# A layer's second attention with its exponent pass five steps behind the scores

## The reference, cut to what matters

```
h = rmsnorm(X, norm1_w)
q, k, v = (h @ wq), (h @ wk), (h @ wv)          # 16 heads of 8 features
scores = einsum('bshd,bthd->bhst', q, k) / sqrt(8)
attn = softmax(scores, axis=-1)                 # no mask here
X = X + einsum('bhst,bthd->bshd', attn, v) @ wo
```

## Time and profile before

| what | value |
|---|---|
| median of 3 runs | 2710.6 us (2710.46 to 2715.17) |
| the profiled execution, its own time | 2712.92 us |
| span of the profile, first to last instruction | 2710.8 us |
| mean granted TensorE clock over the span | 0.887 |
| stage at1, from 701 to 925 us of the span | 8% of the span |
| PE busy, share of the span | 80% |
| DVE, ACT, POOL busy, share of the span | 72%, 51%, 51% |

### The profile page before, as it was taken

The page is one execution under the profiler, slowest core; times in us unless marked ns, Lnnn a source line. Parts: engine busy times, 40 slices in busy tenths (PEclk is TensorE's granted clock), DMA queues, the critical chain, the costliest instruction groups (busy, mean ns, idle before and its releaser), DMA issues. The chain is left out here.

```text
span 2710.8 us, 49483 instructions
## 1 busy us (share of the span) xinstructions
PE 2163.6 (80%) x19467; PEld 1333.7 (49%) x19467; DVE 1956.2 (72%) x3337; ACT 1395.6 (51%) x2141; POOL 1370.4 (51%) x1035
## 2 busy tenths in 40 slices
PE   4999767776378899999889998999999986875703
PEld 1555545554156566666445554555545443553303
DVE  5775547887566466666478888978889885897577
ACT  1556325554266533333277666566666662431496
POOL 3442345555333000000079889898988987664001
PEclk7999878787588899999899999999999999986857
DMA  5431000000344300000022222222222221000001
GB/s 150 98 89 41 1 5 9 9 8 2 77 107 109 93 5 1 1 1 1 23 66 81 77 72 74 71 78 73 85 72 66 77 71 52 16 9 9 0 0 31
DMA packets 130565, 129.51 MB, mean 48 GB/s; under 512 B 21904, under 2 KB 126112, under 8 KB 127136
## 3 DMA queue, kind: packets, MB, share of 16 engines
q1 hardware_dynamic: 126240, 125.56, 16.3%
q10 hardware_dynamic: 4096, 0.79, 0.2%
HBM read 109.73 MB, written 16.58 MB: 47 GB/s over the span
## 5 line engine op out<-in xcount | busy, mean ns | idle before, releaser
L2252 POOL TENSOR_TENSOR mam_h<-mam_h,mam_c_all 128x1024 f32<-128x1024 f32 x256 | 657.1, 2579 | 90.6 <-DVE mam_h L2324 90.6
L2324 DVE TENSOR_TENSOR_SCAN mam_h<-mam_decay,mam_ps_b 128x1024 f32<-128x1024 f32 x256 | 574.5, 2275 | 99.1 <-PE mam_ps_b L1954 97.0
L1954 PEld LDWEIGHTS mam_ps_b<-mam_diag,mam_duT 64*128 64x128 f32 x4096 | 252.9, 191 | 219.2 <-DVE mam_h L2324 129.4
L2144 ACT ACTIVATE mam_decay<-mam_delta,mam_a_neg 128x508 f32<-128x508 f32 x512 | 331.3, 710 | 32.8 <-DVE mam_h L2324 28.6
L1954 PE MATMUL mam_ps_b<-mam_diag,mam_duT 64*128 64x128 f32 x4096 | 298.7, 288 | 54.3 <-DVE mam_h L2324 42.6
L1973 PE MATMUL mam_ps_y<-mam_h,all_ident 64*64 64x512 f32 x2048 | 255.1, 614 | 14.0 <-POOL mam_h L2252 14.0
L792 DVE TENSOR_REDUCE at_top<-at_ps_s 128x4 f32<-128x512 f32 x256 | 169.1, 687 | 116.3 <-PE at_ps_s L521 112.8
L1516 ACT ACTIVATE moe_silu<-moe_ps_g 128x512 f32<-128x512 f32 x144 | 85.9, 597 | 227.1 <-PE moe_ps_g L1459 203.8
L665 ACT ACTIVATE at_e<-at_ps_e 128x512 f32<-128x512 f32 x256 | 145.4, 596 | 91.6 <-PE at_ps_e L521 87.4
L1471 PEld LDWEIGHTS moe_ps_d<-moe_w_down,moe_hidden 128*128 128x128 f32 x1152 | 139.8, 192 | 34.0 <-issue 34.0
L183 POOL TENSOR_TENSOR moe_after_rstd<-moe_after_var,all_minus_half 128x4 f32<-128x4 f32 x8 | 8.1, 1016 | 290.3 <-DVE moe_after_var L178 290.3
(11 more groups left out here) (359 smaller groups left out, 4600.4 us busy)
## 6 DMA issues: line engine op xcount, KB each, us to landing
mam_c_all<-mam_c_rows SPq DMA_DIRECT2D x256, 256.0 KB, 3.4
at_rows<-at_split SPq DMA_DIRECT2D x64, 192.0 KB, 3.0
at_q<-at_rows SPq DMA_DIRECT2D x32, 192.0 KB
at_k<-at_rows SPq DMA_DIRECT2D x32, 192.0 KB
at_q<-at_rows SPq DMA_DIRECT2D x32, 128.0 KB
at_k<-at_rows SPq DMA_DIRECT2D x32, 128.0 KB
all_x_all<-in_x SPq DMA_DIRECT2D x8, 256.0 KB, 4.4
at_q<-at_rows SPq DMA_DIRECT2D x32, 64.0 KB
```

The costliest lines, as they stand in the source:

```text
L1954: last = nc.tensor.matmul(ps_b[:, slot, odd, :, at // 2, x:x + HT], duT[r, d, s % DT, at, :], diag[r, chunk % SLOTS, at, :, :], start=True ...
L2144: last = nc.scalar.activation(decay[:, s % SLOTS, :, n, :, 1:T], src, ACT.Exp, scale=a_neg[:, d, s % DT, st:st + 1])
L2252: nc.gpsimd.tensor_tensor(flat(h[:, slot, :, :, :, :]), flat(h[:, slot, :, :, :, :]), flat(c_all[:, chunk, :, :, :, :]), ALU.mult).then_in ...
L2324: nc.vector.tensor_tensor_scan(row(h[:, s % H_SLOTS, :, :, :, :]), row(decay[:, s % SLOTS, :, :, :, :]), row(ps_b[:, s % 2, :, :, :, :]), ...
```

## The change

For rope=False only, every lag from the exponents on grows by one step. The turning and the output of a group were tied to the places r = 2 and r = 3; they are now found from the lags: LAG_A = G + LAG_U and LAG_O = LAG_A + 1. With rope=True that gives 4, 5, 6, 10, 11, which are the steps of before. With rope=False it gives 5, 6, 7, 11, 12, so the turning of a group's attention comes at r = 3 and its output at r = 0, in the same step as `values_in`. FIRST and LAST stay. The buffers, the rings and SP's order stay.

```
-        LAG_E, LAG_V, LAG_U, LAG_O, LEAD = 4, 5, 6, 2, 2
+        LAG_E, LEAD = 4 if rope else 5, 2
+        LAG_V, LAG_U = LAG_E + 1, LAG_E + 2
+        LAG_A = G + LAG_U
+        LAG_O = LAG_A + 1
...
+        def group_at(s, lag):
+            return (s - lag) // G if (s - lag) % G == 0 and whole((s - lag) // G) else None
...
-            if r == 2 and whole(n - LAG_O):
-                out.append(("a", n - LAG_O))
+            if group_at(s, LAG_A) is not None:
+                out.append(("a", group_at(s, LAG_A)))
             if batch(s - 1):
                 out.append(("t", s - 1))
-            if r == 3 and whole(n - LAG_O):
-                out.append(("o", n - LAG_O))
+            if group_at(s, LAG_O) is not None:
+                out.append(("o", group_at(s, LAG_O)))
...
-                if r == 2 and go:
-                    turn_att(n - LAG_O)
+                if group_at(s, LAG_A) is not None:
+                    turn_att(group_at(s, LAG_A))
...
-                if r == 3 and go:
-                    output(n - LAG_O)
+                if group_at(s, LAG_O) is not None:
+                    output(group_at(s, LAG_O))
```

More of the change, by code:

```diff
@@ L596, in _ @@
                 n, r = s // G, s % G
-                come, go = whole(n + LEAD), whole(n - LAG_O)
+                come = whole(n + LEAD)
                 if r == 1 and come:
@@ L699, in _ @@
                     copy_compact("q", n + LEAD, 0)
-                if r == 2 and go:
-                    take(("a", n - LAG_O), lambda src: nc.scalar.copy(attT[:], src))
+                if group_at(s, LAG_A) is not None:
+                    take(("a", group_at(s, LAG_A)), lambda src: nc.scalar.copy(attT[:], src))
                 if batch(s - LAG_V):
@@ L760, in _ @@
                     before.root(nc, pool, c, n + LEAD + 1)
-                if rope and r == 3 and whole(n - LAG_O):
-                    g = n - LAG_O
+                g = group_at(s, LAG_O)
+                if rope and g is not None:
                     bank, at = AT[("o", g)]
@@ L850, in _ @@
                     find_top(s, 1)
-                if r == 3 and go:
-                    add_x(n - LAG_O)
+                if group_at(s, LAG_O) is not None:
+                    add_x(group_at(s, LAG_O))
                 if r == 0 and whole(n - 1):
```

## The result

| | before | after |
|---|---|---|
| median, interleaved runs | 2712.95 us (10 runs) | 2725.96 us (10 runs) |
| ratio after/before, 95% interval | | 1.0041 (1.003 to 1.0052) |
| profiled execution, its own time | 2712.92 us | 2726.88 us |
| span | 2710.8 us | 2725.1 us |

What follows compares the result with a forecast made beforehand. The prediction took the row-read transfer, in a loop with step 4n's products, to bound stage at1. Terms 1.1 + 1.4 + 3.5 = +6.0 us on the median 2710.6 gave 2716.6 us, range 2710.0 to 2721.0.

Steps and rivals of the forecast that it cites:

- The mechanism: Stage at1: SP's row reads wait for products at step 4n's end, closing a 24.0 us loop; r = 3 waits move to r = 0.
- The transfer: Row reads of a group, from q reads' issue to the next group's first score: taken as 19.8 us.
- first score to step 8: Stage at1's start: step 8 starts where the rows let it, 0.3 us earlier.
- the five periods, step 8 to step 28: Groups 3 to 7: period 24.0 us against 23.73 now, 120.0 us in all; step 28 comes 1.1 us later.
- step 28 to the last addition: Stage's end: slow step 28 costs +1.4 us, one more step of exponents alone +3.5 us.
- the rival that makes the kernel faster: Row reads find the k write landed, transfer shrinks to 17.4 us, period 21.6, result 2704.6 us; chance 0.06.
- slower still: Row reads come later than the products let them: transfer 20.66, period 24.86, result 2720.9 us; chance 0.08.
- The end: Last group: half clock moves to step 28, +1.4 us (0 to 2.5); five steps of exponents alone, +3.5 us.
- The placement of the output: Turning at r = 3, output at r = 0 in step 4n: costed at 0, under 1 us a group without cover.
- The rule of the Trainium skill: K reads with 3, 2 and 1 copies use few engines, so the transfer stays 19.8 us whatever else is in flight.
- The other rivals: Clock stays high in step 4n with shortest transfer, 2709.7 us, chance 0.30 together; transfer shortens, 2704.6 us, chance 0.06.
- The signs: Profile after: no maxima waits at r = 3, group starts 24 us apart, SP's longest wait for exponents, five exponent-only end steps.

Runs made afterwards that it cites:

- experiment 1: Kernel before (lag 4) with only SP's new wait before the row reads added, measured twice: 1.0020 and 1.0032.
- experiment 2: Changed kernel (lag 5) with four slots instead of three for q and k rows in the stage without rotation: 1.0002.
- experiment 3: Kernel before (lag 4) with four slots instead of three for q and k rows in the stage without rotation: 1.0006.
- second profile: The changed kernel run once more, nothing altered, against the kernel before: 1.0052.
- experiment 5: Changed kernel run again, 1.0052; and with SP waiting for the exponents' products before it writes the k rows, 1.0060; both against the kernel before.
- experiment 4: Kernel before (lag 4) with only the turning of a group's attention and its output one step later: 1.0008.
- experiment 6: One DMA for each copy of the k rows, stage at1 only, against the kernel before: 0.9947 on the changed kernel (lag 5), 0.9954 at lag 4.

## Why the prediction was right or wrong

**The mechanism: right, and shown.** The new wait at the row reads closes a loop; the five waits at r = 3 reappear at r = 0. Adding the wait alone costs 5 to 9 us (experiment 1), taking it away at lag 5 wins 10 (experiment 2), and the fourth slot that takes it away does nothing at lag 4 (experiment 3). In steps 12 to 24 the products end 4.10 us after the start, as forecast, SP needs 0.10 to 0.11 us to issue (0.1 forecast), and the granted clock is 0.50 or 0.51.

**The transfer: mis-sized, and this is the step that failed.** It was taken as 19.8 us and as not depending on what SP issues ahead of it. It was 20.67 in the first profile, 20.42 in the second. Part by part, against the one profile of the kernel before (so each part is good to some 2 us, as experiment 2 says), in us:

| | forecast | first profile | second profile |
|---|---|---|---|
| first score to step 8 | -0.3 | -0.85 | -0.75 |
| the five periods, step 8 to step 28 | +1.4 | +5.06 | +4.48 |
| step 28 to the last addition | +4.9 | +6.69 | +6.51 |
| sum | +6.0 | +10.9 | +10.2 |

The largest miss is in the periods. In the first profile five times 0.87 are 4.3 us more than forecast, and 0.7 comes off at step 8, whose products end after 3.41 us and not 4.10: its first products ran at the full clock (granted 1.00 from 769.15 to 769.77) and its last at 0.50 (from 771.53), 0.63 on average. That this equals the 3.41 us of step 12 before is chance, since that step ran at 1.00 and waited for DVE in between. In the second profile step 8 takes 4.10 us too.

The range did hold 20.66 as an upper end, but as a reading of one row and not as something that the change moves. I had argued that a write kept out of the way could only shorten the transfer, and put that as the rival that makes the kernel faster; experiment 5 shows the opposite sign: 19.80 with the write right ahead, 20.67 and 20.42 without. The rival "slower still", with 20.66 and 2720.9 us, had the right term for a reason other than its own, and was given 0.08. There is luck in the 19.8 as well: it is an upper bound for the group that starts at step 8, where both profiles of the changed kernel, with the write 1.3 us ahead in this one group, show 19.40 and 19.39. That it is also the mean of the five later transfers with the write right ahead was not read from any row.

**The end: too small.** Steps 28 to 32 grew from 16.14 to 18.03, +1.9 where 1.4 was forecast, and to 18.76, +2.6, in the second profile, where the half clock lasted longer (the slow step now carries the output and v behind it, which was named and costed at up to 2.5). Steps of exponents alone: 910.88 to 928.65, 17.77 against 13.88, +3.9 in both profiles where 3.5 was forecast; the first of the five has output and v with it. From the last values to the last addition the first profile has 8.10 against 7.19, because its last output ran at the half clock (the window at 933.9). That isn't the change's doing: the second profile has 7.19 and a last output at 1.00, and in experiment 3, with the lags of before, the last output ran at 0.50. In the run with the fourth slot the same stretch, step 28 to the last addition, grew by 6.2.

**The placement of the output** was costed at 0; within the periods experiment 4 bears that out (118.88 against 118.64 us), for the end it leaves up to 4.6 us open. **The rule of the Trainium skill** ("DMA: Bandwidth & Descriptors", Rules for kernel authors: an outermost dimension of c copies confines a DMA to at most c engines): splitting such reads wins 12 to 14 us against the kernel before (experiment 6), which speaks for it; but the length after the split still goes from 13.65 to 19.16 us, so it isn't the whole account, and the split also doubles the number of DMAs, which wasn't tried apart from it. **The other rivals:** the clock did not stay high in steps 12 to 28 (0.50 to 0.55); the transfer did not shorten.

**The signs.** No wait for the maxima and five steps of exponents alone came as put; the group starts are 23.9 to 25.7 us apart, not 24. SP's wait for the exponents' products (2.7 us at most) is not its longest, as I had put it: the waits for maxima to be written to DRAM reach 7.2 us. And the range's lower end, 2710.0, is not the 2709.7 of the case that it names.

## What to carry to other kernels

A lag in a pipeline holds buffers as well as hiding latency: before making consumers later, look for every wait that frees a buffer on their count, and for the queue in which it stands. A wait in the middle of a DMA queue delays all that is behind it, and if what it delays is the longest transfer of the loop, the latency won elsewhere is lost again; here a fourth slot took the wait's cost away, and shortening the transfer itself was worth more than either lag. And cost the drain: each step of lag is one more step at the end with nothing beside it.

## What the runs showed of the hardware

Row reads that started with a write 1.3 us ahead took 19.80 us to the next score (mean of five; 19.86 in a second kernel, where one of the five had it 2.1 us ahead), and 20.67 and 20.42 when the write had been issued 2.4 to 4.0 us earlier; I had expected no difference or the other sign. Split into one DMA for each copy, the same bytes took 13.65 us in one group and 19.16 in another, and for the stage's first group between 12.98 and 18.28 us in five kernels.

The length of PE's wait alone doesn't tell the clock of the next step. Steps 12 to 24 of the changed kernel ran at 0.50 or 0.51 after waits of 3.26 to 5.12 us, and in experiment 2 a step began at 0.50 after 2.29 us (812.18). But the step at 879.70 there, after a wait of 3.60 us, began at 0.97 (its first product takes 0.21 us in the row above, not 0.26) and was at 0.50 from 880.32 on; in the first profile of experiment 1 a step began at 0.92 after 4.17 us and was at 0.50 from its values on.
